# Router, choice and transposes of the combine weights at later steps of an expert chunk

## The reference, cut to what matters

```python
gates = einsum('bsd,ed->bse', x, gate_w)             # x is layer-normalised, 16 experts
scores = sigmoid(gates)
_, inds = top_k(scores + expert_bias, 8)
selected = take_along_axis(scores, inds)
selected = selected / selected.sum(-1) * 2.826       # scattered back to 16 columns: combine
h = silu(einsum('bsd,eid->bsei', x, w_gate)) * einsum('bsd,eid->bsei', x, w_up)
y = einsum('bsed,bse->bsd', einsum('bsei,edi->bsed', h, w_down), combine)
y = y + shared expert(x)                             # a 17th expert without a combine weight
```

## Time and profile before

| | us |
|---|---|
| median of three runs | 1555.93 |
| lowest and highest run | 1554.6, 1556.16 |
| the profiled execution's own time | 1555.15 |
| its span, first to last instruction | 1553.4 |
| PE busy in the span | 1301.2 (84%) |
| DVE busy | 1278.3 (82%) |
| ACT busy | 1096.8 (71%) |
| POOL busy | 900.2 (58%) |

### The profile page before, as it was taken

How to read it: one execution, slowest core, us unless ns; L and a number is a source line. 1 busy time by engine, 2 the same in 40 slices (tenths; PEclk the granted TensorE clock), 3 DMA queues, 4 the chain that set the end, 5 groups by cost and what they waited for, 6 DMA issues and landing times. The chain is left out here.

```text
span 1553.4 us, 21357 instructions
## 1 busy us (share of the span) xinstructions
PE 1301.2 (84%) x6384; PEld 625.0 (40%) x6384; DVE 1278.3 (82%) x2166; ACT 1096.8 (71%) x1578; POOL 900.2 (58%) x1054
## 2 busy tenths in 40 slices
PE   4788878888887699999997787777888489999998
PEld 3344444544443344444443233333333234444443
DVE  2899999999999877878886788888887568777775
ACT  4777777776776355555553899999999955555554
POOL 5899889888978565555565322332222035555555
PEclk9799999999999899999998567878776689999999
DMA  7112112112211043222220000000000022333330
GB/s 245 55 55 109 54 54 105 59 55 68 96 54 55 7 190 131 112 109 109 109 109 1 1 1 0 0 0 0 0 0 1 1 110 116 118 132 143 147 137 26
DMA packets 27924, 111.54 MB, mean 72 GB/s; under 512 B 4050, under 2 KB 9571, under 8 KB 19427
## 3 DMA queue, kind: packets, MB, share of 16 engines
q1 hardware_dynamic: 27010, 110.21, 18.7%
q10 hardware_dynamic: 864, 0.74, 0.1%
HBM read 108.06 MB, written 2.88 MB: 71 GB/s over the span
## 5 line engine op out<-in xcount | busy, mean ns | idle before, releaser
L1042 POOL TENSOR_TENSOR e_h_lo<-e_h,e_h_hi 128x512 f16<-128x512 f32 x272 | 315.0, 1159 | 269.9 <-ACT e_h_hi L1124 257.6
L275 POOL TENSOR_TENSOR m_h<-m_b_sb,m_dx 128x512 f32<-128x512 f32 x256 | 345.6, 1377 | 51.7 <-POOLq L67 40.1
L521 ACT ACTIVATE m_decay<-m_delta,mw_a_log 128x255 f32<-128x255 f32 x448 | 185.3, 461 | 116.9 <-DVEq L695 116.8
L690 DVE TENSOR_TENSOR_SCAN m_h<-m_decay,m_h 128x1024 f32<-128x1024 f32 x112 | 256.0, 2285 | 13.5 <-DVEq L60 7.7
L1119 ACT ACTIVATE e_g<-e_g 128x512 f32<-128x512 f32 x256 | 149.1, 582 | 159.4 <-PE e_g L1064 159.3
L391 PE MATMUL m_y_ps<-m_hc,ident 128*128 128x512 f32 x512 | 260.4, 634 | 0.0
L1621 DVE TENSOR_SCALAR a_d<-a_s 128x512 f32<-128x512 f32 x256 | 170.4, 688 | 56.4 <-PE a_s L1508 37.5
L1064 PE MATMUL e_g<-ef_x_hi,ew_gate_up 128*128 128x512 f16 x544 | 207.6, 382 | 3.8 <-PEq L103 2.4
L1064 PE MATMUL e_u<-ef_x_hi,ew_gate_up 128*128 128x512 f16 x544 | 207.8, 382 | 0.0
L1069 PE MATMUL e_y<-e_h_hi,ew_down 128*128 128x512 f16 x544 | 205.9, 379 | 2.1 <-POOL e_h_lo L1042 2.1
L1124 ACT ACTIVATE e_h_hi<-e_h 128x512 f16<-128x512 f32 x272 | 169.6, 624 | 52.9 <-DVE e_h L1175 51.5
(11 more groups left out here) (234 smaller groups left out, 2038.4 us busy)
## 6 DMA issues: line engine op xcount, KB each, us to landing
e_c_rest<-mix SPq DMA_DIRECT2D x48, 1024.0 KB, 7.1
m_b_sb<-b_rows SPq DMA_DIRECT2D x64, 512.0 KB, 5.4
ef_c_head<-mix SPq DMA_DIRECT2D x16, 1024.0 KB, 4.6
ew_gate_up<-w_gate_up SPq DMA_DIRECT2D x1, 2176.0 KB, 13.6
out<-x_sb SPq DMA_DIRECT2D x8, 256.0 KB, 2.3
ew_down<-w_down SPq DMA_DIRECT2D x1, 1088.0 KB, 11.4
mw_conv_rows<-w_conv_rows ACTq DMA_DIRECT2D x1, 640.0 KB
mix<-ef_cT SPq DMA_DIRECT2D x16, 32.0 KB, 1.6
```

The costliest lines, as they stand in the source:

```text
L275: ins = nc.gpsimd.tensor_tensor(h[:, m % 4, :, c], b_sb[:, p, 2 * m:2 * m + 2], dx[:, p, c:c + 1].to_broadcast([P, 2, T]), ALU.mult)
L521: ins = nc.scalar.activation(decay_of(m, p)[:, at + 1:at + T], delta[:, p, c, 1:T], ACT.Exp, scale=neg_a[:, c, 2 * m + n:2 * m + n + 1])
L690: nc.vector.tensor_tensor_scan(flat, decay_of(m, p)[:], flat, 0.0, ALU.mult, ALU.add).then_inc(scan_chain, 1)
L1042: nc.gpsimd.tensor_tensor(h_lo[:, k], h[:, k], h_hi[:, k], ALU.subtract).then_inc(h_lo_ready, 1)
```

## The change

The router's matmuls and the squash move from step 7 to step 8 of a chunk, the three parts of the choice from steps 8, 9 and 10 to 9, 10 and 11, and the transposes of the combine weights and their reading from step 11 to step 13. Nothing is added or taken away.

```diff
@@ pe body
                         if e == 6:
                             front.transpose_x(pe, t_ps)
-                        if e == 7:
+                        if e == 8:
                             front.route(pe, 1 - p, t_ps)
-                        if e == 11:
+                        if e == 13:
                             front.transpose_comb(pe, t_ps)
@@ dve body
                         if e == 6:
                             front.lower_x(dve, 1 - p, t_ps)
-                        if e in (8, 9, 10):
-                            front.choose(dve, e - 8)
+                        if e in (9, 10, 11):
+                            front.choose(dve, e - 9)
```

## The result

The changed kernel takes 1531.4 us (median of four runs, 1530.63 to 1532.71) against 1555.26 for the kernel before beside it: a ratio of 0.985 (95% interval 0.9838 to 0.9862), 23.9 us less. The forecast was 1531.7. The profiled execution took 1532.71 us, its span is 1531.0.

What follows compares the result with a forecast made beforehand. PE was taken as the bound, 34.62 of 36 us busy, stopping only at router and transposes. Removing both stops saves 24.2 us: 1555.15 to 1530.95, plus 0.78 for the median, 1531.7; range 1529.5 to 1539.

Steps and rivals of the forecast that it cites:

- The two stops and their sum: PE idles before `route` and `transpose_comb`, 14 times each; removing both gains 24.2 us.
- The correction of 0.164 us: Each PE stop costs 0.164 us more than its shown idle time; 28 x 0.164 added to 9.5 + 10.1 us.
- Margins of router and choice: After the move, router data is ready 1.3 us before PE needs it, `ef_comb` 1.2 us before the transposes.
- The combine weights come late: In step 0 of the next chunk DVE waits 0 to 0.9 us for `ef_c_head`.
- The cover of that wait: DVE's delay in step 0 stops PE only from 2.7 us (`up(3)` 2.9, `down(0)` 2.7).
- that DVE makes the lateness up before `normalise`: DVE, free for 7 of 36 us, recovers a step 0 wait of 0.9 us before `normalise`.
- The step "costed at nothing": DVE's wait in step 0 adds no time; without the cover it would cost 0 to 12.6 us.
- The second rival: Combine weights too late in step 0: PE stops from 2.7 us delay, net loss from 4.4; up to 1589 us; slower: 0.05.
- The first rival: POOL holds up the choice on DVE, so the stop at the transposes stays: 1544.2 us; wholly or partly, 0.09.
- The third: The bound passes to another engine, DVE the nearest, and nothing changes: 1556 us; chance 0.04.

Runs made afterwards that it cites:

- single parts undone: Changed kernel with router and choice unmoved (1541.4 us), with the transposes of the combine weights at step 12 (1544.14), or with them at step 11 (1575.56).
- the run at step 14: Changed kernel with the transposes of the combine weights and their reading at step 14 instead of 13: 1540.83 us, ratio 0.9909.
- the run with `read_y` first: Changed kernel with transposes of the combine weights at step 14 and, on ACT in step 2, `read_y` ahead of `upper_h(1)`: 1537.48 us, ratio 0.9891.

## Why the prediction was right

- **The two stops and their sum.** 24.2 us forecast, 23.9 measured. The correction of 0.164 us for each shown idle time was needed: without it the sum would have been 19.6. Chunks of 34.6 us were forecast, 34.63 measured; with single parts undone the chunks came out 0.82, 1.00 and 2.94 us longer, where 0.82, 1.0 and 2.95 were computed.
- **Margins of router and choice.** 1.3 and 1.2 us forecast, 1.27 and 1.08 measured in the chunk shown, at least 1.08 and 0.90 in all.
- **The combine weights come late.** A wait of 0 to 0.9 us was forecast, 0.1 to 1.35 measured. The term that was too small is that from the transposes to the store of `mix`: 1.40 from the earlier trace rows, 1.66 after (1309.41 to 1311.07). On ACT `read_c` now stands behind an `upper_h(12)` that itself waits for DVE, just behind with the choice: it starts 1.00 us behind the transposes, not 0.72. A second term was left out: DVE starts 0.14 us after the load has landed. Together they make 0.40 us; in the chunk shown DVE waited 0.34 longer. The longest wait, 1.35, has the same path at its slowest: 2.10 us from the transposes to the store, and 1.94 from the store to the load.
- **The cover of that wait: wrong.** I put it at 2.7 us, from the banks of `up(3)` and the low half for `down(0)`. Left out was a shorter path, `read_y` behind `upper_h(1)` on ACT (1.5 us by the run at step 14). And that DVE makes the lateness up before `normalise` holds only to 1.8 us, by the run with `read_y` first. The step "costed at nothing" held because the longest wait, 1.35 us, is still under 1.5, by 0.15 and not by the 1.8 that I thought: that a covered wait costs nothing is shown, that this one was covered everywhere is in part luck. In the last chunk of layer 1, with its two bank pairs, the cover is only 0.87 us (at step 14 DVE is 3.22 - 1.20 us late there, and PE stops for 0.99 + 0.16); there the change happened to be late by 0.09. The second rival would so have decided earlier than at 4.4 us: at 1.5 + 1.7 = 3.2.
- **The first rival** (POOL holds up the choice) has the mechanism that it claimed, but with 0.2 us in each chunk as before the change, as said against it, and 0.4 in the first chunk of each layer. Its stop didn't come.
- **The third** (another engine becomes the bound) is out: PE is busy without a gap.

Of the versions without PE's stops, the one with the last two parts of the choice in one step has the same time and DVE's wait covered with more to spare. No kernel run here beats the change by more than the measurement tells.

## What to carry to other kernels

When a producer's steps are moved to give a waiting engine time, compute the margin of every consumer down the chain, and move each consumer by as many steps as its own margin asks: router plus one, transposes plus two; with plus one they still stop, with plus zero they stop three times as long. When a wait is costed at nothing because of a cover, follow all instructions that are queued behind the waiting one on every engine, not only the direct data path: here a queue position on ACT nearly halved the cover. In a trace of pipelined matmuls the idle time of a stop begins at the modelled end of the last matmul, so add what the interval between unhindered matmuls is shorter than the shown duration.

## What the runs showed of the hardware

In the version with the last two parts of the choice together, the last operation of the choice, which reads two SBUF tiles, takes 0.61 to 0.62 us beside POOL's in all 14 chunks and ends 0.08 us behind it; ahead of the layers, where POOL is idle, it takes 0.224 (its durations in ns, min/median/max, and the timeline of POOL and DVE):

```profile
L905 DVE SCALAR_TENSOR_TENSOR ef_comb<-ef_chosen,ef_total x16: 224/618/620, 536.1 to 1479.4; 128x64 f32<-128x64 f32 x16
```

```profile
1305.58 1.16 POOL L1042 TENSOR_TENSOR e_h_lo<-e_h,e_h_hi 128x512 f16<-128x512 f32 x1 [1.20 <-ACT e_h_hi L1124]
...
1306.19 0.62 DVE L905 SCALAR_TENSOR_TENSOR ef_comb<-ef_chosen,ef_total 128x64 f32<-128x64 f32 x1
```

By the rule of the Trainium skill cited ahead (page "SBUF — State Buffer", section "SBUF: two separate sides"), such an operation is held by the lock as one in a two-port mode is, when GpSimd's operation reads SBUF, as this one does; the trace agrees, with 0.62 against 0.224 us. The reduction (0.22 us) and the reciprocal (0.18 us) just ahead of it, with one SBUF input each, ran beside POOL's operation at their usual length.
